# Attention and mixture of experts in one kernel: VectorE's transposes spread over other slices, three splits moved behind the rows' split, early weight loads issued in paced pairs

## The reference

```python
h = jnp.maximum(jnp.einsum('ecd,edh->ech', buf, w1) + b1[:, None, :], 0.0)
out_e = jnp.einsum('ech,ehd->ecd', h, w2) + b2[:, None, :]
gathered = out_e[flat_e, pos_gather]
out_flat = jnp.zeros_like(x_flat).at[flat_t].add(gathered * w_eff[:, None])
```

## Time and profile before

| | us |
|---|---|
| median of 3 runs | 1977.08 |
| lowest, highest | 1974.52, 1977.10 |
| the profiled execution's own time | 1976.32 |
| its span, first to last instruction | 1974.7 |
| PE busy | 1926.3 (98%) |
| DVE busy | 1139.0 (58%) |
| POOL busy | 807.9 (41%) |
| ACT busy | 738.0 (37%) |
| DMA, mean | 88 GB/s |

### The profile page before, as it was taken

One profiled execution on the slowest core, in us unless ns is written; L12 is line 12 of the kernel. 1 busy time (PEld: TensorE's weight loads), 2 busy tenths in 40 slices (PEclk: granted clock), 3 DMA queues, 4 the chain that ended last, 5 costly groups with the idle time before them and its releaser, 6 DMA issues.

```text
span 1974.7 us, 35688 instructions
## 1 busy us (share of the span) xinstructions
PE 1926.3 (98%) x10114; PEld 1700.6 (86%) x10115; DVE 1139.0 (58%) x2102; ACT 738.0 (37%) x1233; POOL 807.9 (41%) x972
## 2 busy tenths in 40 slices
PE   8999999999999999999999999999999999999998
PEld 7899999997888888898889888888888888988887
DVE  5467787867545655556554635645536545546453
ACT  4434444444323433343333423433324323423332
POOL 2122236375554454444435333354433333433543
PEclk9999999999999999999999999999999999999999
DMA  7245455457122421242114304321133133133211
GB/s 174 92 123 166 147 163 156 124 164 217 23 38 50 146 60 27 43 153 58 26 37 119 95 16 95 96 65 26 41 115 96 37 96 110 28 90 96 67 27 26
DMA packets 150990, 174.05 MB, mean 88 GB/s; under 512 B 40366, under 2 KB 94766, under 8 KB 150928
## 3 DMA queue, kind: packets, MB, share of 16 engines
q1 hardware_dynamic: 120560, 134.16, 22.2%
q0 software_dynamic: 30368, 39.11, 11.1%
HBM read 124.33 MB, written 53.11 MB: 90 GB/s over the span
## 4 chain that ended last, share of the span: by engine, by line
PE 93%; DVE 3%; issue 2%; ACT 1%; DMA 1%; POOL 0%; POOLq 0%; SPq 0%; DVEq 0%
PE bank L1655 18%; PE bank L1659 17%; PE bank L1658 17%; PE pair_v L1655 7%; PE pair_v L1659 7%; PE pair_v L1658 7%; PE pair_o L1659 5%; PE pair_o L1655 5%; PE pair_o L1658 5%; PE bank L1881 1%; DVE xq L1141 1%; PE pair_v L1977 1%; PE pair_o L1977 1%; PE bank L1665 1%; DVE h_hi L1169 1%
## 5 line engine op out<-in xcount | busy, mean ns | idle before, releaser
L1169 DVE CAST h_hi<-h 128x512 fp32r<-128x512 f32 x320 | 144.5, 451 | 644.6 <-ACT h L887 491.7
L675 POOL DMA_INDIRECT xg<-normed,quad_rows x304 | 320.5, 1054 | 388.7 <-PE pair_v L1659 302.6
L1655 PE MATMUL bank<-w_hi,h_hi 128*128 (+1 forms) x752 | 294.8, 392 | 4.9 <-DVE h_lo L1171 4.7
L1658 PE MATMUL bank<-w_lo,h_hi 128*128 (+1 forms) x752 | 295.3, 393 | 1.2 <-issue 1.2
L1659 PE MATMUL bank<-w_hi,h_lo 128*128 (+1 forms) x752 | 295.1, 392 | 0.3 <-issue 0.3
L887 ACT ACTIVATE h<-bank,b_cur 128x512 f32<-128x512 f32 x160 | 110.4, 690 | 491.8 <-PE bank L1659 456.3
L708 POOL DMA_INDIRECT out_dram<-ys,tab_s x80 | 129.5, 1619 | 372.2 <-DVE ys L1162 352.1
L887 ACT ACTIVATE h<-pair_v,b_cur 128x512 f32<-128x512 f32 x160 | 110.4, 690 | 411.3 <-PE pair_v L1659 391.9
L1655 PE MATMUL bank<-et_hi,w_hi 128*128 128x384 f32 (+5 forms) x640 | 227.2, 355 | 21.8 <-issue 21.0
L1171 DVE TENSOR_TENSOR h_lo<-h,h_hi 128x512 fp32r<-128x512 f32 x320 | 222.0, 694 | 11.0
L1655 PE MATMUL pair_v<-et_hi,w_hi 128*128 128x384 f32 (+5 forms) x640 | 225.1, 352 | 1.7 <-issue 1.6
(11 more groups left out here) (281 smaller groups left out, 3807.4 us busy)
## 6 DMA issues: line engine op xcount, KB each, us to landing
w_raw<-L_ffn_w_dram SPq DMA_DIRECT2D x128, 512.0 KB, 4.9
xb<-_attn_hidden_states_dram SPq DMA_DIRECT2D x32, 256.0 KB, 3.4
xr<-_attn_hidden_states_dram SPq DMA_DIRECT2D x32, 256.0 KB
out_dram<-x SPq DMA_DIRECT2D x32, 256.0 KB
normed<-x1n SPq DMA_DIRECT2D x32, 256.0 KB
x_quads<-xn SPq DMA_DIRECT2D x21, 256.0 KB, 2.5
xn<-x_quads SPq DMA_DIRECT2D x21, 256.0 KB, 3.9
a_quads<-at SPq DMA_DIRECT2D x21, 256.0 KB
```

The costliest lines, as they stand in the source:

```text
L675: nc.gpsimd.indirect_dma_start(out=xg[:, h, P * a:P * (a + 1)], out_offset=None, in_=normed_quads, in_offset=bass.IndirectOffsetOnAxis(ap= ...
L1169: ve_.tensor_copy(h_hi[:, mm % 4, :], h32[:, mm % 2, :]).then_inc(h_split_hi, 1)
L1655: ins = mm_(out_, lh, rh, start=(first and c == 0), stop=False, skip_group_check=shared)
L1658: mm_(out_, lh, rl, start=False, stop=False, skip_group_check=shared)
```

## The change

It has three parts. TURN_AT moves the four transposes from slices 12, 13, 14, 15 to slices 8, 10, 12, 14. The w1 split that stood in slice 15 (slice RING - 1 = 3 of the next tile) is made in `tile_end` behind the four pieces of the rows' split, on both engines, and the w2 split of pair 4 moves from slice 15 of a `split` tile to slice 0 of the next tile. SP issues the early loads from w1 pair 5 and w2 pair 3 on in steps, each behind a wait for first products of tile 0.

```diff
-        TURN_AT = {12 + h: h for h in range(BT)}
+        TURN_AT = {8 + 2 * h: h for h in range(BT)}
-        W2_AT = {2 * j + 7: j for j in range(5)}
+        W2_AT = {2 * j + 7: j for j in range(4)}
...
             load_w1(0, 4)
             load_w2(0, 2)
-            load_w1(0, 5)
-            load_w2(0, 3)
-            load_w1(0, 6)
-            load_w2(0, 4)
-            load_w1(0, 7)
-            for j in range(5, PAIRS):
+            for j in range(3, PAIRS):
+                sp.wait_ge(h_full, 2 * j - 4)
+                if j < 6:
+                    load_w1(0, j + 2)
                 load_w2(0, j)
             sp.wait_ge(plan_ready, 1)
...
-                    if mm + RING < MC or not last:
+                    if mm + RING < MC or not last and mm < MC - 1:
                         w1_split(e + 1 if split and mm + RING >= MC else e, g, mm + RING)
...
                 rows_hi(g + 1, 3)
+                w1_split(e + 1 if split else e, g + 1, RING - 1)
                 if split:
                     b1_load(e + 1, g + 1)
                 for mm in range(RING):
                     relu(g + 1, mm)
                     w1_split(e + 1 if split else e, g + 1, mm + RING)
-                    if split and mm > 0:
+                    if split:
                         w2_split(e + 1, mm + 4)
...
-                w1_split(0, 0, mm + RING)
+                if mm < MC - 1:
+                    w1_split(0, 0, mm + RING)
...
-                    if mm + RING < MC or not last:
+                    if mm + RING < MC or not last and mm < MC - 1:
                         w1_lo_part(g, mm + RING)
...
                 rows_lo(g + 1, 3)
+                w1_lo_part(g + 1, RING - 1)
                 y_weighted(g)
                 for mm in range(RING):
                     hidden(g + 1, mm)
                     w1_lo_part(g + 1, mm + RING)
-                    if split and mm > 0:
+                    if split:
                         w2_lo_part(e + 1, mm + 4)
...
-                w1_lo_part(0, mm + RING)
+                if mm < MC - 1:
+                    w1_lo_part(0, mm + RING)
```

## The result

The changed kernel takes 1964.26 us, the median of 4 runs (1962.54 to 1967.45), beside 1977.09 for the kernel before in the same session (4 runs, 1974.52 to 1980.4). The profiled execution is the slowest of the four, 1967.45 with a span of 1965.8, so the two traces differ by 8.9 us and not by 12.8.

What follows compares the result with a forecast made beforehand. PE was taken to bound the kernel, with 1926.3 us of work in a 1974.7 span. Part 1 gave -7.0, Parts 2 and 3 gave 0: 1976.3 to 1969.3, taken as 1969.6 between two bases; range 1965 to 1977.

Steps and rivals of the forecast that it cites:

- Part 1: Tile 0: pacing SP's early loads in pairs removes PE's idle time in slices 4 and 5; -7.0 us, bounds 0 and 7.6.
- late data: Tile 0: whether the paced w1 and w2 loads land too late for their splits; cost 0, with slices as cover.
- the holes: PE's pauses between matmuls in slices 4 and 5 of tile 0, 7.6 us excess, read as instruction fetches late behind loads.
- a crowd must last to hurt: Tile 0: inferred because 440 to 450 us had a DMA share of 0.95 with no hole.
- Rival A: Tile 0: the holes stay because any traffic when a fetch is due suffices; all 7.6 us may stay, 1976.3; 16%.
- The rule set against it: Tile 0: crossing a 16 KiB instruction block is mostly hidden; then pacing would give 0 and the time stay 1976.3.
- Part 3: Slice 15 and tile end: splits behind the rows' split let et_lo start 2.3 us earlier, PE not noticing; 0.
- Part 2: Transposes moved to slices 8, 10, 12, 14, none removed; gathers cost 0, gain 0, bounds 0 and 6.5 us.
- the question of h_lo: Whether PE's 0.54 us waits for slice 15's h_lo in 12 tiles go; slice 14 keeps its transpose, so gain 0.
- Rival B: Tile ends improve as well: all 12 waits of 0.54 us for h_lo go, 1962.8; 8%.
- Rival C: Tile heads after expert changes: slipped w1 pair 1 load lengthens PE's gaps, 7 x 1.62 = 11.3 us, 1980.6; 8%.
- extra w2 split at slice 0: Next tile after an expert change, seven times: at most 1.22 us delay against 3.9 us to spare; cost 0.

Runs made afterwards that it cites:

- e3: Kernel before with only TURN_AT changed, transposes in slices 8, 10, 12, 14, splits and loads as before: 1955.51 us, ratio 0.9942.
- e1: Kernel before with only SP's early loads paced as in the change: 1967.66 us, ratio 1.0004 to the kernel before.
- e5: The changed kernel itself, unaltered, run again on a chip without holes: 1957.01 us, ratio 0.9952 to the kernel before.
- e4: Kernel before with only PE's wait for et_ready moved behind the branches, next to the first product: 1955.65 us, ratio 0.994.
- e7: Changed kernel with the four transposes two slices earlier, behind slices 6, 8, 10 and 12: 1949.8 us, ratio 0.9911 to the kernel before.
- e9: Changed kernel with PE reading an expert's word of the plan once instead of twice: 1949.33 us, ratio 0.9911 to the kernel before.

## Why the prediction was wrong

**The direction and rough size of the time came out, by the wrong path.** I gave 7.0 us to pacing and 0 to all else; it was 0 and about 10 to 12. Two errors of opposite sign nearly cancelled, which is luck.

**Part 1, -7.0: the step that failed is the inference** that PE's instructions come late behind the loads. The loads went in steps with a gap, and "late data" cost 0 as said: no wait for w_lo appeared. But the holes stayed at full length with the DMA engines idle (8.5 us of excess in the kernel after, where the forecast left 0.6), and pacing alone, on a chip without holes, measured 1.0004. The warning was in my own text: a share of 1.05 without a hole, 0.75 with one. I saved the reading with "a crowd must last to hurt", a clause made to fit two rows. e3 then held 12 us of crowd without a hole, on another chip. Rival A was right that the holes stay, though not in its reason. The rule set against it, from the Trainium skill (Runtime: NRT & Kernel Launch, section Instruction fetch mechanics), that crossing a block of instructions is mostly hidden, gives 0 for pacing. e1 agrees with it; it leaves the holes of the first chip unexplained.

The trace could have tested the inference, for it records the packets that carry instructions. In the kernel after, 480 to 483 us have one of them, and 483 to 494 us have only loads and scatters (packets, MB, share of the 16 engines; the first line is from 480 to 483, the other two are all the queues of 483 to 494):

```profile
q8 instruction: 1, 0.02, 2.7%
...
q1 hardware_dynamic: 629, 0.73, 21.0%
q0 software_dynamic: 202, 0.01, 1.5%
```

The packet of 16 KB took about 1.3 us (2.7% of 16 engines in 3 us). PE's two longest holes, 1.60 and 1.00 us, came behind it, and at 490.06 PE went on at full load with no instruction packet in between. So as far as these packets are recorded, PE did not wait for a fetch there. In the kernel before, the packet came at 488 to 490, at the end of the holes and some 7 us later in the tile than in e3, so by itself that trace would have let the inference stand. Whose instructions a packet carries is not named.

What the rows do show is another sign that I passed over. ScalarE stood idle beside the holes with its input done. Kernel after, the last matmul of slice 4's first product, and ScalarE's first work on it:

```profile
477.43 0.39 PE L1661 MATMUL bank<-et_hi,w_lo 128*128 128x512 f32 x1
...
489.81 0.69 ACT L885 ACTIVATE h<-bank,b_cur 128x512 f32<-128x512 f32 x1 [12.89 <-remote]
```

That is 12.0 us; in the kernel before it is 11.9, and in e5 ScalarE takes the same product as soon as it is done.

**Part 3, 0: this is the second failed step, and the one that cost the range.** "et_lo can then start behind h_lo, at 620.40, 2.3 us earlier, and PE, busy with last_blocks, does not notice: 0." The size of the shift was right for tile 2: et_lo from 622.69 to 620.07, 2.6 us, of which 0.25 is the whole tile's earlier place in the trace. The cover was not. I compared et_lo's end, 625.19, with the first matmul at 627.20 and took the 2.0 between them for slack. It was PE's own work behind its wait. PE was busy, but its sequencer stood at the wait, and the engine ran dry. I had written that the heads are "where PE's sequencer reads the plan and branches; the diff leaves that code alone", and did not ask when that code could start. The diff did not touch it, but set its start. e4 shows it from the other side.

**Part 2.** The gathers' cost of 0 was right, and so was the question of h_lo: slice 14 kept its transpose and the 12 waits stayed (4.7 to 4.5 us). Its upper bound, 6.5 us, was a good price, for another edit: e7 moved that transpose away and won 7.2. But I cost the move only against h_lo. Slice 15's transpose stands ahead of et_lo, and moving the transposes alone gave the whole gain (e3).

**Rival B** came close to the time (1962.8 forecast, 1964.26 measured) with a mechanism that did not happen. **Rival C** fell: the pause at the head of tile 3 went from 2.13 to 2.01 us, and those at ordinary heads to none. VectorE's and ScalarE's extra w2 split at slice 0, costed at 0, shows in no wait.

**The range** was too narrow for one reason: the heads had no bound of their own. Rows 3 had 21.3 us of "issue"; bounded by what could come back at ordinary heads, 7.0 us, the forecast of 1969.6 would have had 1962.6 inside its range, and so the measured 1964.26. Three smaller terms were off too. A quiet slice 4 takes 5.54 us and not 5.44, so the holes were 7.5 us. A stretch at half clock cost 0.8 to 1.1 us, not 1.7. And rival C in full, 1980.6, lay under its own mark for slower, 1981.0.

**Still open.** What makes the holes of tile 0 on the one chip. Nor is it shown why the result's chip gave 12.8 us and the chip of e5 9.5 for the same pair of kernels; the intervals, 0.9916 to 0.9956 and 0.9938 to 0.9965, overlap. Why pauses at the changes of expert keep up to 2.0 us beside the read is not divided further. Pacing alone was not run on a chip with holes; there, only the trace of the kernel after speaks.

## What to carry to other kernels

Where a consumer's first instruction comes a constant time behind its producer in many tiles of one kind, that time is work behind the consumer's wait and not slack, even where the profile calls the idle time "issue". Put the wait as near as possible to the instruction that needs it, or have the producer done that much earlier; one of them is enough. A coincidence in one stretch of one execution, such as holes beside a crowd of loads, is to be held against a second stretch with the same crowd, and if possible another chip, before microseconds are put on it.

## What the runs showed of the hardware

- 1.97 to 2.50 us pass on PE's sequencer between a satisfied wait and the first matmul, for a semaphore increment, a loop's entry, two more waits and two nested levels of branches: 2.50 us in tiles 4, 7, 12 and 19 of the kernel before, where four tests are passed over, and 0.23 to 0.27 less with each test fewer. With the wait moved inside there is no pause with et_lo ended 1.5 us ahead of the first product (e4).
- The Trainium skill (Runtime: NRT & Kernel Launch, section Instruction fetch mechanics) says that a taken branch to a place outside the fetched pages waits for a fetch. This trace does not show it at these heads: in 750 to 765 us of the kernel before, around the head of tile 4 with its 2.50 us, the only queue with packets is the one of GpSimd's scatters, and none carries instructions.

```profile
q0 software_dynamic: 144, 0.00, 0.5%
```

- One `value_load` of a word of on-chip memory into PE's registers, left out ahead of a tile's head, saved 0.65 to 0.70 us, eight times out of eight (e9 beside e5).
- The same kernel showed in tile 0 two holes on one chip, in both kernels, and none on three others. They cost 7.5 us in the kernel before and 8.5 in the changed one (7.05 and 12.46 against 5.54 and 5.44); that chip was 10 us slower on the kernel before and 7 on the changed one (beside e5). While they last, VectorE and ScalarE run dry as well. In the kernel after ScalarE's waits from 470 to 520 us:

```profile
ACT h L885 <- remote: 20.8, 3, 12.9
```
